# Gate and up of eight expert blocks as three fp32r terms, in a four-layer transformer stage

## The chip, the cores and the metric

The kernel runs on one core of a Trainium2 chip. The metric is device time in microseconds, the median of three runs. A profile of one execution stands beside it: it has every instruction's start and duration on each engine, the DMA issues, and the clock that TensorE was granted. Engines are named PE (TensorE), DVE (VectorE), ACT (ScalarE), POOL (GpSimd) and SP (SyncE, which here only issues DMAs).

## The reference

An activation of 4 x 256 tokens with 256 channels passes through four layers. Each layer forms a gated, decayed two-way scan ("cond") of the activation and feeds it to a feed-forward part, whose result is added. The third layer's feed-forward part is the one that matters here, a mixture of 8 experts with 2 chosen per token:

```python
def _L2_ffn_ref(hidden_states, gate_weight, gate_up_proj, down_proj):
    B, S, H, I, E, K = (4, 256, 256, 512, 8, 2)
    router_logits = x @ gate_weight.T
    probs = softmax(router_logits)
    top_v, top_i = top_k(probs, 2)
    ...
    def expert_step(acc, inp):
        gu, dp, w = inp
        gate, up = jnp.split(x @ gu.T, 2, axis=-1)
        hidden = silu(gate) * up
        y = hidden @ dp.T
        return (acc + w[:, None] * y, None)
```

The fourth layer's feed-forward part multiplies by three weight matrices that are first rounded to -1, 0 and 1 by their own mean ("ternary" weights).

## The kernel before

The eight experts' tokens are sorted by expert into blocks of 128 rows, at most 23 blocks (`NB`). The second expert loop works on one block at a time. A block `b` gathers its 128 rows from memory (POOL, `gather_block`), turns them on PE (`turn_block`) and copies them to `xbT` (ACT, `block_turned`). `gate` and `up` multiply `xbT` by the two halves of the expert's weights `gu`, 256 x 1024 numbers or 1 MB, which SP loads per block into a ring of three slots (`up_weights`, L375 to L379). ACT takes the silu of gate, DVE multiplies it by up (`block_h`), PE turns the product (`turn_block_hidden`) and multiplies it by the down weights (`block_down`), ACT copies the result out of PSUM (`block_y`), and POOL scatters it (`scatter_block`).

The order on each engine is written out by hand. On PE, iteration `b` is: gate of `b`, turning of the hidden rows of `b-1`, turning of the input rows of `b+1`, up of `b`, down of `b-1`. All operands of these matmuls are fp32; the profile shows each fp32 matmul as two records of the same shape.

DVE and POOL have other work in the same iterations. In the first 16 blocks DVE runs two scans per block for the fourth layer's cond (`late_scan`), POOL adds them up (`late_sum`, `late_value`), and every second block DVE takes a reciprocal and a product (`gain_reciprocal`, `gain_out`). And the three ternary weight matrices are prepared one after the other in one buffer, `traw` of 1 MB: SP loads it (`ternary_in`), DVE sums its magnitudes (`ternary_sum`, block 2, 8 or 14), PE adds over partitions (`ternary_total`) and DVE rounds (`ternary_round`, block 4, 10 or 16), DVE clips (`ternary_clip`, block 5, 11 or 17), and POOL writes the result as bf16 (`ternary_write`, block 6, 12 or 18). The next matrix can be loaded only after that write. SP's queue is in order: `ternary_in` of the second and third matrix stands right behind `up_weights(8)` and `up_weights(14)`, and it waits for the POOL write before it, so that `up_weights(9)` and `up_weights(15)` stand behind that wait:

```python
for b in range(2, NB):
    ...
    up_weights(b)
    if b in (8, 14):
        ternary_in((1, 8, 14).index(b))
```

In the first layer another expert loop already multiplies in three fp32r terms: with `mm3` each fp32 operand is given as a high part in fp32r and a low remainder, and high x high, high x low and low x high are added up.

Of the kernel before, what the change touches and what calls it, by code (L numbers as in the profile page):

```python
# [56 lines left out]
COPIED = {"": 0, "3": NT - 1}  # L57
LANED = 13
SUMMED = {"place": 1, "rows": 2, "dest": 3}
RANKED = [(0, 4, 0), (4, 2, 2), (6, 2, 3)]  # L60
# [8 lines left out]
def build(nc, x_d, kt_d, te_d, w_d, u_d, sm_d, gbias_d, down_d, fc2_d, w1_d, w2_d,  # L69
          q1_d, q1b_d, q2_d, q2b_d, rt_d, gu_d, dn_d, t1_d, t2_d, t3_d, cond_d, y_d, cw_d, out_d):  # L70
    with ExitStack() as ctx:
# [21 lines left out]
        kT = sb("kT", [P, NBLK, S])  # L93
        ekk = sb("ekk", [P, NBLK, 2, S])
        GT = sb("GT", [P, 2, NBLK, S])
        eu = sb("eu", [P, 2, 2, S])
        fw = sb("fw", [P, 2, 2, S])
        bw = sb("bw", [P, 2, 2, S])
        cond = sb("cond", [P, NT, C])
        turned = cursor[0]  # L100
# [12 lines left out]


        cursor[0] = turned
        cwb = sb("cwb", [P, CRING, TOK])
# [60 lines left out]
        gu = sb("gu", [P, RING, KC, 2 * I2])  # L177
        region2 = cursor[0]


# [7 lines left out]
        hm = sb("hm", [P, 2, I2])  # L188
        hT2 = sb("hT2", [P, 2, I2 // P, P])
        lane_of = sb("lane_of", [P, 2 * NT, P], F16)  # L190
        slab_of = sb("slab_of", [P, 2 * NT, NBW], F16)
        slab_val = sb("slab_val", [P, 2 * NT, NBW], F16)
        r2c = sb("r2c", [P, 2, NT, E2 * E2], BF16)
        xbT = sb("xbT", [P, 2, KC, P])
        slot_end = cursor[0]
        ends.append(cursor[0])


# [97 lines left out]
        def latent_bank(v):  # L296
            return bank[(4, 6, 2, 7)[v]]

        def unit(u):
# [15 lines left out]
        def _(sp):  # L315
# [16 lines left out]
            def expert_w1(eg):  # L332

                wait(sp, sem("w1_split"), eg - 1)
                sp.dma_start(w1raw[:, eg % 2, :], w1_d[:, eg, :]).then_inc(sem(f"w1_in{eg % 2}"), 16)
# [58 lines left out]
            for b in range(2, NB):  # L394
                if b == 2:
                    sp.wait_ge(sem("xb_in2"), 16)
                up_weights(b)
                if b in (8, 14):
                    ternary_in((1, 8, 14).index(b))
            sp.wait_ge(sem("y_out0"), 16 * ((NB + 1) // 2))  # L400
# [10 lines left out]
        def _(pool):  # L411
# [94 lines left out]
            def split_w1(eg):  # L506

                wait_alone(f"w1_in{eg % 2}", 16 * (eg // 2 + 1))
                wait_alone("z_ready", 8 * eg - 8)
                pool.tensor_scalar(w1hi[:, eg % 2, :], w1raw[:, eg % 2, :], 1.0, 0.0, ALU.mult, ALU.add).then_inc(sem("w1_high"), 1)  # L510
                wait_alone("w1_high", eg + 1)
                pool.tensor_tensor(w1lo[:, eg % 2, :], w1raw[:, eg % 2, :], w1hi[:, eg % 2, :].bitcast(F32), ALU.subtract
                                   ).then_inc(sem("w1_split"), 1)

# [104 lines left out]
            for b in range(NB):  # L619
                if b + RING < NB:  # L620
                    gather_block(b + RING)
                if b == 2:
                    pool.wait_ge(sem("routed"), ROUTED["dest"])
                if b >= 2:
                    scatter_block(b - 2)
                if b < 2 * NBLK:
                    late_sum(b // 2, 1 - b % 2, ("den", "num")[b % 2])
                    if b % 2 and b // 2 + 1 < NBLK:
                        late_value(b // 2 + 1)
                if b in (6, 12, 18):  # L630
                    ternary_write((6, 12, 18).index(b))
                if b in (19, 20):
                    combine_rows(b - 19)
# [50 lines left out]
        def _(act):  # L684
# [225 lines left out]
            def block_turned(b):  # L910

                act.wait_ge(sem("xbt_ready"), b + 1)
                wait(act, sem("up_done"), b - 1)
                act.activation(xbT[:, b % 2, :, :], xb_bank(b), ACT.Copy).then_inc(sem("xbT_ready"), 1)  # L914

# [92 lines left out]
        def _(dve):  # L1008
# [98 lines left out]
            def cond_low(n0, s, k):  # L1107
                n = n0 + 2 * s + k
                dve.wait_ge(sem("cT_high"), n + 1)
                dve.tensor_tensor(cTlo[:, k, HALF * s:HALF * s + HALF], cond_bank(n)[:],  # L1110
                                  cThi[:, k, HALF * s:HALF * s + HALF].bitcast(F32), ALU.subtract
                                  ).then_inc(sem("cT_low"), 1)

# [375 lines left out]
            def ternary_round(m):  # L1489
                dve.wait_ge(sem("tsum_ready"), m + 1)  # L1490
                dve.tensor_scalar(ws[:, 15 + m:16 + m], total_bank(4 + 6 * m), 1.0 / (C * HID), 1e-5, ALU.mult, ALU.max
                                  ).then_inc(sem("tsum_read"), 1)
# [13 lines left out]
            def late_scan(i, part):  # L1506
# [6 lines left out]
                else:  # L1513
                    dve.tensor_tensor_scan(bw[:, p, d, S - 2::-1], ekk[:, i, d, S - 1:0:-1], col(decf, n).to_broadcast([P, S - 1]),
                                           0.0, ALU.add, ALU.mult).then_inc(sem("scan_num" if part == 3 else "scan_den"), 1)

            for b in range(NB):
# [88 lines left out]
        def _(pe):  # L1606
# [22 lines left out]
            def turn_cond(l, n0, s):  # L1629
                pe.wait_ge(sem("cond_ready"), 4 * l + 2 * s + 2)  # L1630
                for k in range(KC):
                    n = n0 + 2 * s + k
                    wait(pe, sem("cT_low"), n - 1)
                    for j in range(TH):
# [95 lines left out]
            pe.wait_ge(sem("sm_low"), 2)  # L1730
            pe.wait_ge(sem("cT_low"), 2)
            scores_up(bank[6], E0, sm_hi, sm_lo, 0)
# [4 lines left out]
            shared_up(0)  # L1737
            pe.wait_ge(sem("cT_low"), 4)
            pe.wait_ge(sem("xl_low"), 1)
# [6 lines left out]
            def expert_z(u):  # L1746
# [6 lines left out]
                if u % 8 == 0:  # L1753
                    pe.wait_ge(sem("w1_split"), e // 4 + 1)
                mm3(bank[u % 4][:], (w1hi[:, slot, w], w1lo[:, slot, w]),
# [205 lines left out]
            def ternary_total(m):  # L1961
                pe.wait_ge(sem("tsum_part"), m + 1)
                pe.matmul(total_bank(4 + 6 * m), ones[:], ws[:, 9 + m:10 + m], start=True, stop=True).then_inc(sem("tsum_ready"), 1)

            def turn_block(b):

                pe.wait_ge(sem(f"xb_in{b % RING}"), 16 * (b // RING + 1))
                wait(pe, sem("xbT_ready"), b)
                for k in range(KC):
                    ins = pe.transpose(xb_bank(b)[:, k * P:k * P + P], xb[:, b % RING, k * P:k * P + P], ident[:])  # L1970
                ins.then_inc(sem("xbt_ready"), 1)

            def gate(b):
# [6 lines left out]
                wait(pe, sem("hm_ready"), b - 1)  # L1980
                if b in (4, 10, 16):
                    ternary_total((4, 10, 16).index(b))
                for k in range(KC):
                    ins = pe.matmul(bank[2 * (b % 2)][:], xbT[:, b % 2, k, :], gu[:, b % RING, k, 0:I2],  # L1984
                                    start=(k == 0), stop=(k == KC - 1))
                ins.then_inc(sem("gate_done"), 1)

            def up(b):

                if b == HALVED:  # L1990
                    pe.wait_ge(sem(f"gu_in{b % RING}"), 16)
                if b in (4, 10, 16):
                    pe.wait_ge(sem("tsum_read"), (4, 10, 16).index(b) + 1)
                for k in range(KC):
                    ins = pe.matmul(bank[2 * (b % 2) + 1][:], xbT[:, b % 2, k, :], gu[:, b % RING, k, I2:2 * I2],  # L1995
                                    start=(k == 0), stop=(k == KC - 1))
                ins.then_inc(sem("up_done"), 1)

# [149 lines left out]
```

## Time and profile before

| | |
|---|---|
| median of 3 runs | 446.32 us (446.3 to 446.4) |
| profiled execution, its own time | 446.5 us |
| its span, first to last instruction | 444.7 us |
| mean granted TensorE clock | 0.972 |
| PE busy | 400.8 us, 90% of the span |
| DVE busy | 328.9 us, 74% |
| POOL busy | 253.7 us, 57% |
| ACT busy | 236.9 us, 53% |
| bytes moved | 69.52 MB, mean 156 GB/s |

The second expert loop runs from about 248 to 384 us of the span. The profile's lists name a line of the kernel, an engine, an operation and the tiles that it writes and reads. L1984 is gate, L1995 is up, L2006 is the turning of the hidden rows, L2028 is down, L1504 is `block_h`, L1512 and L1514 are the late scans, L602, L606 and L597 are POOL's sums and value for them, L571 is the ternary write, L361 is the load of `traw` and L378 that of a block's weights. Ends of matmuls are modelled, so the pace of PE is read from starts.

### The profile page before, as it was taken

Reading aid. Unit: us, or ns where it says so; the run is one execution under the profiler, and the core shown is the slowest. Engines: PE = TensorE matmul, PEld = TensorE weight load, DVE = VectorE, ACT = ScalarE, POOL = GpSimd, SP = SyncE. Lnnn points to the kernel's source line nnn. Section 1 sums busy time; section 2 is a strip of 40 time slices with the busy share of each in tenths; the row PEclk is TensorE's granted clock in tenths of the full one; section 3 lists DMA queues with packets and bytes.
Section 4 is the critical chain, followed back from the end, with each engine's and each line's share of the span. In section 5 each row is a group of like instructions: output and inputs, shape, how many; then the busy total and the mean of one; then the engine's idle time right before and its main releaser. Section 6 shows DMA issues by size and latency. Waiting matters only on the chain.

```text
span 444.7 us, 6082 instructions
## 1 busy us (share of the span) xinstructions
PE 400.8 (90%) x1749; PEld 264.2 (59%) x1749; DVE 328.9 (74%) x620; ACT 236.9 (53%) x478; POOL 253.7 (57%) x352
## 2 busy tenths in 40 slices
PE   7798999999899999968894899999999999976895
PEld 7576788555455555636682466666666666653553
DVE  5998788999999999889978278548546411058993
ACT  6624683566676667658975222333333332249882
POOL 5474018578788997244622567876985562124641
PEclk9999999999999999997995999999999999999998
DMA  6910006366456656062023786496587760140011
GB/s 216 414 38 0 1 1 209 114 218 199 152 186 204 219 173 223 10 272 109 2 95 109 239 308 212 170 353 222 222 303 254 249 226 24 44 170 0 25 35 36
DMA packets 21439, 69.52 MB, mean 156 GB/s; under 512 B 3136, under 2 KB 7616, under 8 KB 17952
## 3 DMA queue, kind: packets, MB, share of 16 engines
q1 hardware_dynamic: 18112, 62.07, 39.8%
q0 software_dynamic: 2208, 6.03, 4.1%
q10 hardware_dynamic: 1088, 1.05, 0.7%
q8 instruction: 14, 0.23, 0.2%
q14 instruction: 17, 0.14, 0.1%
HBM read 63.90 MB, written 5.24 MB: 155 GB/s over the span
## 4 chain that ended last, share of the span: by engine, by line
PE 50%; DVE 27%; issue 12%; POOL 4%; ACT 3%; DMA 3%; SPq 0%; DVEq 0%; POOLq 0%; ACTq 0%
PE bank L1984 9%; PE bank L2028 9%; PE bank L1995 9%; PE bank L1764 5%; DVE hx L1289 5%; DVE fw L1078 4%; DVE bw L1081 3%; PE bank L1609 2%; PE bank L1611 2%; PE bank L1610 2%; PE bank L2006 2%; DVE fw L1086 2%; PE bank L1686 2%; DVE gl L1568 2%; PE bank L1861 2%
## 5 line engine op out<-in xcount | busy, mean ns | idle before, releaser
L1764 PE MATMUL bank<-hx,w2raw 128*128 128x512 f32 x128 | 67.2, 607 | 4.1 <-DVE hx L1289 3.3
L1504 DVE TENSOR_TENSOR hm<-bank,sl 128x512 f32<-128x512 f32 x23 | 15.8, 689 | 62.6 <-PE bank L1995 34.5
L802 ACT ACTIVATE rl<-bank 128x512 f32<-128x512 f32 x64 | 38.1, 595 | 38.8 <-PE bank L1611 37.7
L1609 PE MATMUL bank<-xlhi,w1hi 128*128 128x512 f32 x64 | 49.4, 772 | 0.0
L1289 DVE TENSOR_TENSOR hx<-bank,cwb 128x512 f32<-128x512 f32 x64 | 42.1, 660 | 3.1 <-ACT bank L806 3.1
L2028 PE MATMUL bank<-dn,hT 128*128 x184 | 43.6, 380 | 0.5 <-ACT hT L925 0.5
L1984 PE MATMUL bank<-gu,xbT 128*128 128x512 f32 x92 | 43.6, 596 | 0.5 <-ACT xbT L914 0.5
L2028 PEld LDWEIGHTS bank<-dn,hT 128*128 128x128 f32 x184 | 34.9, 190 | 14.8 <-issue 11.3
L1995 PE MATMUL bank<-gu,xbT 128*128 128x512 f32 x92 | 43.3, 593 | 0.0
L931 ACT ACTIVATE yb<-bank 128x256 f32<-128x256 f32 x23 | 8.8, 383 | 60.9 <-PE bank L2028 60.9
L583 POOL DMA_INDIRECT y_rows<-yb,dest_i x23 | 23.7, 1029 | 30.9 <-ACT yb L931 26.7
L1086 DVE RECIPROCAL fw<-fw 128x256 f32<-128x256 f32 x23 | 39.8, 1732 | 0.0
L806 ACT ACTIVATE bank<-rl 128x512 f32<-128x512 f32 x64 | 38.1, 597 | 0.0
L478 POOL TENSOR_TENSOR fw<-fw,bw 128x256 f32<-128x256 f32 x32 | 24.4, 761 | 15.6 <-DVE bw L1081 15.2
L919 ACT ACTIVATE sl<-bank 128x512 f32<-128x512 f32 x23 | 13.7, 597 | 33.5 <-PE bank L1984 33.5
L1764 PEld LDWEIGHTS bank<-hx,w2raw 128*128 128x128 f32 x128 | 22.4, 188 | 15.2 <-DVE hx L1289 9.7
L1078 DVE TENSOR_TENSOR_SCAN fw<-bank,ekk 128x256 f32<-128x256 f32 x46 | 31.1, 677 | 0.2
L576 POOL DMA_INDIRECT xb<-cond_rows,row_i x23 | 27.6, 1201 | 5.9 <-issue 1.9
L1081 DVE TENSOR_TENSOR_SCAN bw<-ekk,bank 128x255 f32<-128x255 f32 x46 | 30.8, 669 | 0.0
L475 POOL TENSOR_TENSOR eu<-eu,kT 128x256 f32<-128x256 f32 x16 | 11.7, 730 | 25.9 <-ACT eu L700 25.5
L482 POOL TENSOR_TENSOR fw<-fw,eu 128x256 f32<-128x256 f32 x32 | 23.7, 741 | 3.5
L1610 PE MATMUL bank<-xllo,w1hi 128*128 128x512 f32 x64 | 25.3, 395 | 0.0
(307 smaller groups left out, 955.2 us busy)
## 6 DMA issues: line engine op xcount, KB each, us to landing
gu<-in_gu SPq DMA_DIRECT2D x22, 1024.0 KB, 5.3
cwb<-cw_rows SPq DMA_DIRECT2D x32, 512.0 KB, 4.1
dn<-in_dn SPq DMA_DIRECT2D x4, 1024.0 KB, 7.8
traw<-in_t SPq DMA_DIRECT2D x3, 1024.0 KB, 5.0
w1raw<-in_w SPq DMA_DIRECT2D x8, 256.0 KB, 4.9
w2raw<-in_w SPq DMA_DIRECT2D x8, 256.0 KB, 4.4
kT<-in_kt SPq DMA_DIRECT2D x4, 256.0 KB, 4.5
x<-in_x SPq DMA_DIRECT2D x2, 512.0 KB, 7.0
```

Source lines behind the costliest of these rows:

```text
L802: act.activation(rl[:, u % 3, :], bank[u % 4][:], ACT.Relu).then_inc(sem("r_ready"), 1)
L806: act.activation(bank[u % 4][:], rl[:, u % 3, :], ACT.Square).then_inc(sem("sq_ready"), 1)
L1078: dve.tensor_tensor_scan(fw[:, p, d, :], decay(NBLK * l + blk, S), ekk[:, blk, d, :], 0.0, ALU.mult, ALU.add)
L1081: dve.tensor_tensor_scan(bw[:, p, d, S - 2::-1], ekk[:, blk, d, S - 1:0:-1], decay(NBLK * l + blk, S - 1), 0.0, ALU.add, ALU.mult).then_in ...
L1086: dve.reciprocal(fw[:, p, 1, :], fw[:, p, 1, :]).then_inc(sem("rden_ready"), 1)
L1289: dve.tensor_tensor(hx[:, 0, u % 4, :], bank[u % 4][:], cwb[:, e % CRING, HALF * s:HALF * s + HALF], ALU.mult).then_inc(sem("h0_ready"), 1)
L1609: pe.matmul(out, lhs[0], rhs[0], start=start, stop=False)
L1610: pe.matmul(out, lhs[0], rhs[1], start=False, stop=False)
L1764: pe.matmul(bank[4 + s][:], w2raw[:, e // 4 % 2, e % 4, :], hx[:, 0, u % 4, :], start=(e == 0), stop=(e == E0 - 1), skip_group_check=True) ...
L1984: ins = pe.matmul(bank[2 * (b % 2)][:], xbT[:, b % 2, k, :], gu[:, b % RING, k, 0:I2], start=(k == 0), stop=(k == KC - 1))
L1995: ins = pe.matmul(bank[2 * (b % 2) + 1][:], xbT[:, b % 2, k, :], gu[:, b % RING, k, I2:2 * I2], start=(k == 0), stop=(k == KC - 1))
L2028: ins = pe.matmul(y_bank(b), hT2[:, b % 2, j, :], own_down(b, j), start=(j == 0), stop=(j == 3))
```

## The change

In eight blocks, 6, 12 and 17 to 22, gate and up are computed with `mm3`. The high parts of the two halves of the weights are made by ACT (`weights_high`), one block ahead: the gate half at the start of its iteration, the up half after `block_turned`. DVE makes the low parts (`weights_low`, a subtraction that writes over the weights' own ring slot) and the low part of the rows (`block_low`, from PSUM); all of it stands around `block_h` of the block before. The high parts lie in two buffers over tiles that are idle then. The ternary steps move one block earlier: sums at blocks 1, 7 and 13, rounds at 3, 9 and 15, clips at 4, 10 and 16, writes at 5, 11 and 17, and the loads of the second and third matrix stand behind `up_weights(7)` and `up_weights(13)`. Some semaphores are merged and renamed.

```diff
+SPLIT = (6, 12, 17, 18, 19, 20, 21, 22)
+SUM_AT, ROUND_AT, CLIP_AT, WRITE_AT = (1, 7, 13), (3, 9, 15), (4, 10, 16), (5, 11, 17)
...
                 up_weights(b)
-                if b in (8, 14):
-                    ternary_in((1, 8, 14).index(b))
+                if b in SUM_AT[1:]:
+                    ternary_in(SUM_AT.index(b))
...
-                if b in (6, 12, 18):
-                    ternary_write((6, 12, 18).index(b))
+                if b in WRITE_AT:
+                    ternary_write(WRITE_AT.index(b))
...
+            def weights_high(b, up):
+
+                n = slice(up * I2, up * I2 + I2)
+                i = SPLIT.index(b)
+                act.wait_ge(sem(f"gu_in{b % RING}"), 16 * (b // RING + 1))
+                act.wait_ge(sem("up_done"), SPLIT[i - 2] + 1 if i >= 2 else 1)
+                act.activation(gu_high(b)[:, :, n], gu[:, b % RING, :, n], ACT.Copy).then_inc(sem("weights_high"), 1)
...
             for b in range(NB + 1):
+                if b + 1 in SPLIT:
+                    weights_high(b + 1, 0)
                 if b < NB:
                     block_silu(b)
...
                 if b + 1 < NB:
                     block_turned(b + 1)
+                if b + 1 in SPLIT:
+                    weights_high(b + 1, 1)
...
+            def weights_low(b, up):
+
+                n = slice(up * I2, up * I2 + I2)
+                dve.wait_ge(sem("weights_high"), halves_low(b, up))
+                dve.tensor_tensor(gul[:, b % RING, :, n], gu[:, b % RING, :, n], gu_high(b)[:, :, n].bitcast(F32), ALU.subtract
+                                  ).then_inc(sem("weights_low"), 1)
+
+            def block_low(b):
+
+                dve.wait_ge(sem("xbT_ready"), b + 1)
+                dve.tensor_tensor(xbl[:, b % 2, :, :], xb_bank(b).rearrange("p (k n) -> p k n", k=KC),
+                                  xbh[:, b % 2, :, :].bitcast(F32), ALU.subtract).then_inc(sem("turned_low"), 1)
+
             for b in range(NB):
-                if b in (4, 10, 16):
-                    ternary_round((4, 10, 16).index(b))
+                if b in ROUND_AT:
+                    ternary_round(ROUND_AT.index(b))
                 if b < 2 * NBLK:
                     late_scan(b // 2, 2 * (b % 2))
                     late_scan(b // 2, 2 * (b % 2) + 1)
+                if b + 1 in SPLIT:
+                    weights_low(b + 1, 0)
+                    block_low(b + 1)
                 block_h(b)
+                if b + 1 in SPLIT:
+                    weights_low(b + 1, 1)
                 if b >= 2 and b <= 2 * NBLK and b % 2 == 0:
                     gain_reciprocal(3 * NBLK + b // 2 - 1, (b // 2 - 1) % 2)
                     gain_out(3 * NBLK + b // 2 - 1, 3, b // 2 - 1, (b // 2 - 1) % 2)
...
-                if b in (2, 8, 14):
-                    ternary_sum((2, 8, 14).index(b))
-                if b in (5, 11, 17):
-                    ternary_clip((5, 11, 17).index(b))
+                if b in SUM_AT:
+                    ternary_sum(SUM_AT.index(b))
+                if b in CLIP_AT:
+                    ternary_clip(CLIP_AT.index(b))
...
+            def half_product(b, up):
+
+                n = slice(up * I2, up * I2 + I2)
+                for k in range(KC):
+                    if b in SPLIT:
+                        ins = mm3(bank[2 * (b % 2) + up][:], (xbh[:, b % 2, k, :], xbl[:, b % 2, k, :]),
+                                  (gu_high(b)[:, k, n], gul[:, b % RING, k, n]), k == 0, k == KC - 1)
+                    else:
+                        ins = pe.matmul(bank[2 * (b % 2) + up][:], xbT[:, b % 2, k, :], gu[:, b % RING, k, n],
+                                        start=(k == 0), stop=(k == KC - 1))
+                return ins
```

## Rows read from the trace of the kernel before

**Rows 1.** Busy time by stretch: window, length, then each engine's, clock, DMA.
```profile
248.50:380.00 131.50, 131.50 (x495) 81.99 (x496) 68.76 (x98) 39.99 (x110) 85.37 (x99) 1.00 0.65 230
...
433.50:436.90 3.40, 1.61 (x13) 1.07 (x11) 2.99 (x8) 1.46 (x4) 1.62 (x5) 1.00 0.04 15
436.90:440.30 3.40, 3.25 (x16) 2.74 (x16) 0.95 (x2) 0.93 (x3) 0.00 (x0) 0.51 0.08 27
```

**Rows 2.** Timeline of PE in the loop, blocks 16 to 18: start, length, instructions.
```profile
350.10 1.89 PE L2028 MATMUL bank<-dn,hT 128*128 x8
351.82 1.88 PE L1984 MATMUL bank<-gu,xbT 128*128 128x512 f32 x4
353.54 0.60 PE L2006 MATMUL bank<-ident,hm 128*128 128x128 f32 x4
...
354.20 1.88 PE L1995 MATMUL bank<-gu,xbT 128*128 128x512 f32 x4
```

**Rows 3.** Timeline of PE in the first layer's expert loop, one unit.
```profile
150.22 1.02 PE L1764 MATMUL bank<-hx,w2raw 128*128 128x512 f32 x2
...
151.55 0.40 PE L1611 MATMUL bank<-xlhi,w1lo 128*128 128x512 f32 x1
151.78 1.02 PE L1764 MATMUL bank<-hx,w2raw 128*128 128x512 f32 x2
```

**Rows 4.** Groups by line: count, busy us, mean ns. DVE subtractions' nearest, ACT's split.
```profile
L1247 DVE TENSOR_TENSOR rt<-rt 128x256 f32<-128x256 f32 x1 | 0.4, 426 | 0.0
L1230 DVE TENSOR_TENSOR rt<-rt 128x64 f32<-128x64 f32 x1 | 0.2, 228 | 0.0
L775 ACT ACTIVATE sm_hi<-sm_raw 128x1344 fp32r<-128x1344 f32 x1 | 1.3, 1307 | 0.0
```

**Rows 5.** Timeline of DVE in blocks 4 and 5 of the loop.
```profile
277.07 0.69 DVE L1512 TENSOR_TENSOR_SCAN fw<-dec,ekk 128x256 f32<-128x256 f32 x1
277.68 0.66 DVE L1514 TENSOR_TENSOR_SCAN bw<-ekk,dec 128x255 f32<-128x255 f32 x1
...
280.71 1.27 DVE L1498 TENSOR_SCALAR traw<-traw 128x2048 f32<-128x2048 f32 x1
```

**Rows 6.** Timeline of POOL in blocks 5 and 6 of the loop.
```profile
278.59 0.74 POOL L602 TENSOR_TENSOR fw<-fw,bw 128x256 f32<-128x256 f32 x1
...
280.16 0.73 POOL L597 TENSOR_TENSOR eu<-euk,kT 128x256 f32<-128x256 f32 x1
...
285.69 1.90 POOL L571 TENSOR_SCALAR tw<-traw 128x2048 bf16<-128x2048 f32 x1
```

**Rows 7.** Timeline of SP's DMA issues after the first ternary write.
```profile
287.61 0.34 SPq L361 DMA_DIRECT2D traw<-in_t  x1
288.71 3.45 SPq L378 DMA_DIRECT2D gu<-in_gu  x2
```

**Rows 8.** DMA landings: issues at 288.71 and 323.83, us from issue to landing.
```profile
gu<-in_gu SPq DMA_DIRECT2D x1, 1024.0 KB, 7.8
...
gu<-in_gu SPq DMA_DIRECT2D x1, 1024.0 KB, 9.9
```

**Rows 9.** Timeline of PE where the gate of block 8 starts.
```profile
293.20 1.88 PE L1984 MATMUL bank<-gu,xbT 128*128 128x512 f32 x4
```

**Rows 10.** Timelines of POOL and DVE in the first expert loop, two meetings.
```profile
148.04 1.00 POOL L478 TENSOR_TENSOR fw<-fw,bw 128x256 f32<-128x256 f32 x1
...
148.05 0.41 DVE L1092 SCALAR_TENSOR_TENSOR GT<-fw 128x256 f32<-128x256 f32 x1
...
89.02 0.98 DVE L1092 SCALAR_TENSOR_TENSOR GT<-fw 128x256 f32<-128x256 f32 x1
```

**Rows 11.** Timeline of DVE in block 16 of the loop.
```profile
344.65 0.69 DVE L1504 TENSOR_TENSOR hm<-bank,sl 128x512 f32<-128x512 f32 x1 [2.69 <-PE bank L1995]
345.26 1.74 DVE L1086 RECIPROCAL fw<-fw 128x256 f32<-128x256 f32 x1
347.11 0.42 DVE L1092 SCALAR_TENSOR_TENSOR GT<-fw 128x256 f32<-128x256 f32 x1
```

More of the change, by code:

```diff
@@ L94, in build @@
         ekk = sb("ekk", [P, NBLK, 2, S])
+        gt_at = cursor[0]
         GT = sb("GT", [P, 2, NBLK, S])
@@ L98, in build @@
         bw = sb("bw", [P, 2, 2, S])
+        cond_at = cursor[0]
         cond = sb("cond", [P, NT, C])
@@ L112, in build @@
         assert cursor[0] <= turned + KC * TOK * 4
+        cursor[0] = gt_at
+        guh0 = sb("guh0", [P, KC, 2 * I2], F32R)
+        assert cursor[0] <= gt_at + NBLK * S * 4
+        cursor[0] = cond_at
+        guh1 = sb("guh1", [P, KC, 2 * I2], F32R)
+        assert cursor[0] <= turned
         cursor[0] = turned
@@ L178, in build @@
         region2 = cursor[0]
+        cursor[0] = first_region
+        gul = sb("gul", [P, RING, KC, 2 * I2], F32R)
+        assert cursor[0] == region2
         cursor[0] = region
@@ L189, in build @@
         hT2 = sb("hT2", [P, 2, I2 // P, P])
+        lanes_at = cursor[0]
         lane_of = sb("lane_of", [P, 2 * NT, P], F16)
@@ L193, in build @@
         r2c = sb("r2c", [P, 2, NT, E2 * E2], BF16)
+        turned_at = cursor[0]
         xbT = sb("xbT", [P, 2, KC, P])
@@ L196, in build @@
         ends.append(cursor[0])
+        cursor[0] = turned_at
+        xbh = sb("xbh", [P, 2, KC, P], F32R)
+        assert cursor[0] == slot_end
+        cursor[0] = lanes_at
+        xbl = sb("xbl", [P, 2, KC, P], F32R)
+        assert cursor[0] <= lanes_at + 2 * NT * P * 2
         cursor[0] = first_region
@@ L297, in latent_bank, with gu_high, halves_low, rows_low @@
             return bank[(4, 6, 2, 7)[v]]
+        def gu_high(b):
+            return (guh0, guh1)[SPLIT.index(b) % 2]
+        def halves_low(b, up):
+            return EG + 2 * SPLIT.index(b) + up + 1
+        def rows_low(b):
+            return 4 + SPLIT.index(b) + 1
         def unit(u):
@@ L332, in expert_w1 @@
             def expert_w1(eg):
-                wait(sp, sem("w1_split"), eg - 1)
+                wait(sp, sem("weights_low"), eg - 1)
                 sp.dma_start(w1raw[:, eg % 2, :], w1_d[:, eg, :]).then_inc(sem(f"w1_in{eg % 2}"), 16)
@@ L509, in split_w1 @@
                 wait_alone("z_ready", 8 * eg - 8)
-                pool.tensor_scalar(w1hi[:, eg % 2, :], w1raw[:, eg % 2, :], 1.0, 0.0, ALU.mult, ALU.add).then_inc(sem("w1_high"), 1)
-                wait_alone("w1_high", eg + 1)
+                pool.tensor_scalar(w1hi[:, eg % 2, :], w1raw[:, eg % 2, :], 1.0, 0.0, ALU.mult, ALU.add).then_inc(sem("weights_high"), 1)
+                wait_alone("weights_high", eg + 1)
                 pool.tensor_tensor(w1lo[:, eg % 2, :], w1raw[:, eg % 2, :], w1hi[:, eg % 2, :].bitcast(F32), ALU.subtract
-                                   ).then_inc(sem("w1_split"), 1)
+                                   ).then_inc(sem("weights_low"), 1)
             split_w1(0)
@@ L913, in block_turned @@
                 wait(act, sem("up_done"), b - 1)
-                act.activation(xbT[:, b % 2, :, :], xb_bank(b), ACT.Copy).then_inc(sem("xbT_ready"), 1)
+                act.activation((xbh if b in SPLIT else xbT)[:, b % 2, :, :], xb_bank(b), ACT.Copy).then_inc(sem("xbT_ready"), 1)
+            def weights_high(b, up):
[4 more added lines that the diff above has]
+                act.activation(gu_high(b)[:, :, n], gu[:, b % RING, :, n], ACT.Copy).then_inc(sem("weights_high"), 1)
             def block_silu(b):
@@ L1111, in cond_low @@
                                   cThi[:, k, HALF * s:HALF * s + HALF].bitcast(F32), ALU.subtract
-                                  ).then_inc(sem("cT_low"), 1)
+                                  ).then_inc(sem("turned_low"), 1)
             def xl_low(s):
@@ L1490, in ternary_round @@
                 dve.wait_ge(sem("tsum_ready"), m + 1)
-                dve.tensor_scalar(ws[:, 15 + m:16 + m], total_bank(4 + 6 * m), 1.0 / (C * HID), 1e-5, ALU.mult, ALU.max
+                dve.tensor_scalar(ws[:, 15 + m:16 + m], total_bank(ROUND_AT[m]), 1.0 / (C * HID), 1e-5, ALU.mult, ALU.max
                                   ).then_inc(sem("tsum_read"), 1)
@@ L1515, in late_scan @@
                                            0.0, ALU.add, ALU.mult).then_inc(sem("scan_num" if part == 3 else "scan_den"), 1)
+            def weights_low(b, up):
+                n = slice(up * I2, up * I2 + I2)
+                dve.wait_ge(sem("weights_high"), halves_low(b, up))
+                dve.tensor_tensor(gul[:, b % RING, :, n], gu[:, b % RING, :, n], gu_high(b)[:, :, n].bitcast(F32), ALU.subtract
+                                  ).then_inc(sem("weights_low"), 1)
+            def block_low(b):
+                dve.wait_ge(sem("xbT_ready"), b + 1)
+                dve.tensor_tensor(xbl[:, b % 2, :, :], xb_bank(b).rearrange("p (k n) -> p k n", k=KC),
+                                  xbh[:, b % 2, :, :].bitcast(F32), ALU.subtract).then_inc(sem("turned_low"), 1)
             for b in range(NB):
-                if b in (4, 10, 16):
-                    ternary_round((4, 10, 16).index(b))
+                if b in ROUND_AT:
+                    ternary_round(ROUND_AT.index(b))
                 if b < 2 * NBLK:
@@ L1632, in turn_cond @@
                     n = n0 + 2 * s + k
-                    wait(pe, sem("cT_low"), n - 1)
+                    wait(pe, sem("turned_low"), n - 1)
                     for j in range(TH):
@@ L1730, in _ @@
             pe.wait_ge(sem("sm_low"), 2)
-            pe.wait_ge(sem("cT_low"), 2)
+            pe.wait_ge(sem("turned_low"), 2)
             scores_up(bank[6], E0, sm_hi, sm_lo, 0)
@@ L1737, in _ @@
             shared_up(0)
-            pe.wait_ge(sem("cT_low"), 4)
+            pe.wait_ge(sem("turned_low"), 4)
             pe.wait_ge(sem("xl_low"), 1)
@@ L1753, in expert_z @@
                 if u % 8 == 0:
-                    pe.wait_ge(sem("w1_split"), e // 4 + 1)
+                    pe.wait_ge(sem("weights_low"), e // 4 + 1)
                 mm3(bank[u % 4][:], (w1hi[:, slot, w], w1lo[:, slot, w]),
@@ L1962, in ternary_total @@
                 pe.wait_ge(sem("tsum_part"), m + 1)
-                pe.matmul(total_bank(4 + 6 * m), ones[:], ws[:, 9 + m:10 + m], start=True, stop=True).then_inc(sem("tsum_ready"), 1)
+                pe.matmul(total_bank(ROUND_AT[m]), ones[:], ws[:, 9 + m:10 + m], start=True, stop=True).then_inc(sem("tsum_ready"), 1)
             def turn_block(b):
@@ L1968, in turn_block @@
                 wait(pe, sem("xbT_ready"), b)
+                if b - 1 in SPLIT:
+                    pe.wait_ge(sem("turned_low"), rows_low(b - 1))
                 for k in range(KC):
@@ L1980, in gate @@
                 wait(pe, sem("hm_ready"), b - 1)
[L1981 to L1985, printed above, removed]
+                if b in ROUND_AT:
+                    ternary_total(ROUND_AT.index(b))
+                if b in SPLIT:
+                    pe.wait_ge(sem("turned_low"), rows_low(b))
+                    pe.wait_ge(sem("weights_low"), halves_low(b, 0))
+                ins = half_product(b, 0)
                 ins.then_inc(sem("gate_done"), 1)
@@ L1991, in up @@
                     pe.wait_ge(sem(f"gu_in{b % RING}"), 16)
[L1992 to L1997, printed above, removed]
+                if b in ROUND_AT:
+                    pe.wait_ge(sem("tsum_read"), ROUND_AT.index(b) + 1)
+                if b in SPLIT:
+                    pe.wait_ge(sem("weights_low"), halves_low(b, 1))
+                half_product(b, 1).then_inc(sem("up_done"), 1)
             def turn_block_hidden(b):
```

## The prediction, made before the changed kernel was run

> **What bounds the kernel now.** I read the busy time by stretch first. In the second expert loop PE is busy 131.5 of 131.5 us at full clock, while DVE is busy 69 and ACT 40 of them [rows 1]. The timeline of PE in one iteration then gives the pieces, by starts: down takes 1.72 us (350.10 to 351.82), gate 1.72, the two turnings together 0.66, up 1.72 like gate [rows 2]. That is 5.82 us per block with no gap, so a microsecond taken from PE here is a microsecond off the end, as long as operands come in time. Next I read what feeds PE: the issues on SP's queue with their landings [rows 7, 8], and the DVE and POOL instructions that decide when SP may issue [rows 5, 6].
>
> **What it removes on PE.** Gate is four fp32 records in 1.72 us, 0.43 each [rows 2]. For the new terms I use the first expert loop: one unit, two fp32 records and three fp32r terms, takes 151.78 - 150.22 = 1.56 us; less 0.86 for the two records this leaves 0.70, or 0.23 per term, and the last term's start to the next start is 0.23 too [rows 3]. Each of those terms loads its own weights, as the new ones do. Gate becomes six terms, 1.39 us, and saves 0.33; up the same. Eight blocks with two halves make 16 x 0.33 = 5.3 us. From below, a term whose weight load were not covered would eat the saving from 1.72 / 6 = 0.287 us on; no row has such a term. The Trainium skill ("TensorE: Matmul & The Clock Gate", Back-to-back issue gap) gives a pace of N/2.4 + 2.5 ns, 216 ns for 512 columns. By that figure the saving would be 16 x 0.42 = 6.8 us, and my sum 1.5 us less; the row has 0.23, and the measurement decides.
>
> **What it adds on ACT and DVE.** An ACT copy of 1344 elements per partition from fp32 to fp32r took 1.31 us [rows 4]; two of 1024 are 2.1 us per split block. A DVE operation with two SBUF inputs took 0.43 us for 256 elements and 0.23 for 64, 1.03 ns per element, so that 1024 take 1.22 us (estimate from these two rows) [rows 4]; two of these and 0.43 for `block_low` are 2.9 us. In blocks 17 to 22 DVE has little else, and a split block still takes PE 5.16 us: I cost this work at nothing there, covered by that time; without cover it would be at most DVE's sum, 0.7 + 2.9 us against 5.2, so still nothing. `weights_high` waits for the block's weights at the head of ACT's queue, with silu behind it; the weights land about a block earlier, so nothing.
>
> One place is tight. In iteration 16 DVE has, from the start of `block_h`: 0.69, `weights_low` 1.22, reciprocal 1.74, product 0.42, the clip of 1.27 that now stands here, `weights_low` 1.22 and `block_low` 0.43, together 7.0 us, or 6.6 if neighbours overlap as 344.65 to 345.26 do [rows 5, 11]. From there PE is ready for gate 18 after about 6.6 (1.72 + 1.39 + 0.66 + 1.39 + 1.72, less 0.3 that `block_h` starts late). The ternary write of 1.90 us [rows 6] may then hold up the next `weights_low`. I take a loss of 0.5 us, between 0.2 and 0.8.
>
> **What it moves: the weights of blocks 8 and 14.** This is where I expect the saving to go. The second ternary load now stands before `up_weights(8)` on SP. It waits for the POOL write of the first matrix, and that write waits for more than before. Step by step, on the clock of the trace before, whose blocks up to 5 keep their times:
> - The clip used to come in an iteration without reciprocal; now it comes in iteration 4, where the scans start today: 277.07 to 278.34. The scans of block 5 follow, ending 279.6 instead of 278.34 [rows 5].
> - POOL's sums and value for them stand before the write in iteration 5. They start 0.25 us after the scans and take 280.89 - 278.59 = 2.30, to 282.15; the write of 1.90 ends at 284.05, if nothing holds POOL up [rows 6].
> - Something does. When DVE ran a 0.41 us product of two SBUF tiles, a POOL sum that had started with it took 1.00 instead of 0.74 and ended 0.58 after DVE; where POOL came first, the same DVE product took 0.98 [rows 6, 10]. So the two wait for each other. `weights_low(6, 0)` runs from 279.5 to 280.75, right when POOL's first sum wants to start: it ends at 281.35 instead of 280.6, 0.75 late. `weights_low(6, 1)`, ready at about 281.6, slips in after the second sum and costs the value step another 0.95. The write ends at 285.75.
> - `traw` is issued then, and `up_weights(8)` 1.1 us behind it, at 286.85 [rows 7]. In this position the weights landed 7.8 and 9.9 us after issue, behind the megabyte of `traw` [rows 8]: 294.65 to 296.75. I take 8.3, 295.15, nearer the first.
> - Gate 8 starts at 293.20 today [rows 9]; block 6 brings it 0.66 forward, to 292.54. PE waits 2.6 us, between 2.1 and 4.2.
>
> The clip at 10, block 12 and `up_weights(14)` repeat this pattern. Two waits are 5.2 us (4.2 to 8.4). Before the change the same transfers had a block more of time.
>
> A wait of this length has a second price. In 433.5 to 436.9 PE was busy 1.61 of 3.4 us at full clock, and the next 3.4 us ran at 0.51, the lower level of 1.2 GHz [rows 1]. In those, PE does about 1.7 us less work. Of the two waits I let one be followed by such a fall: 1.7 us, between 0 and 3.4.
>
> The rule in the Trainium skill that speaks against this change is in "SBUF — State Buffer", Who interferes with whom: a DVE instruction with two SBUF inputs and a GpSimd instruction that reads SBUF exclude each other for the whole instruction, and `tensor_tensor` is named. By that rule the four steps above wait in full, 1.7 us per event as I have it; had the trace's meetings been a matter of the scalar product alone, the sum would be that of the first rival. No row here has a DVE `tensor_tensor` of that length beside POOL.
>
> **The sum.** -5.3 + 5.2 + 0.5 + 1.7 = +2.1 us. The profiled execution took 446.5 us itself (span 444.7 and 1.8 around it), so 448.6; it lies 0.2 over the median of the runs, 446.32, so the forecast for the median is 448.4. From the terms' bounds the forecast case goes from 445.4 (-5.3 + 4.2 + 0.2) to 453.6.
>
> **Rivals.**
> - *POOL isn't held up.* If `weights_low` and POOL's sums run side by side, the write ends at 284.05, the weights at 285.15 + 8.3 = 293.45 (292.95 to 295.05), and each wait is 0.9 us (0.4 to 2.5), too short for a fall of the clock. Then -5.3 + 1.8 + 0.2 = -3.3: 443.0, faster. For it: POOL's sum at 278.59 and later ones show a steady 0.72 to 0.74 beside other DVE work. Against it: the two meetings above. It decides from the point where both waits together stay under 4.8 us, that is, gate 8 starts before about 295.
> - *The weights come in time altogether.* Should `traw` and the weights both land within 6.8 us of the issue at 285.75, only the 0.2 remains: 441.2. The rows have 8.9 and 11.0 for such a pair (1.1 + 7.8 and 1.1 + 9.9), so it is unlikely.
> - *The backlog is as at 323.83, and both waits drop the clock.* 8.4 + 0.8 + 3.4 - 5.3 = +7.3: 453.6.
> - *The terms don't save what they should.* With 0.287 us per term nothing is gained and the late weights meet a PE that is no earlier: 2 x 2.0 + 0.5 = +4.5: 450.8. The 64 such units of the first loop speak against it.
>
> **How the numbers follow.** Forecast case 0.57, POOL not held up 0.23, weights in time 0.07, backlog with both falls 0.10, terms without gain 0.03. About 0.2%, 0.9 us, is what a measurement of this kernel can tell from no change, so "same" is 445.4 to 447.2. The first rival and the second give faster, 0.30. Of the forecast case some 0.12 lies within the bound (short waits, no fall), and 0.45 above; with the last two, slower is 0.58 and same 0.12. For 8 times in 10 the range leaves out the weights in time and the far part of the backlog case: 442.4 to 452.0. Since both signs are in it, the likeliest case's own: 446.3 to 450.6.
>
> **What would show it.** In the changed trace: gate and up of the eight blocks at 1.39 us by starts; the other pieces as they are. The write of the first matrix ending near 285.75 (284.05 for the first rival), POOL's first sum in block 5 near 1.5 us instead of 0.74. PE idle before the gates of blocks 8 and 14, ended by the DMA of `gu`, for 2.1 to 4.2 us each, and a small one at gate 18 ended by DVE. A clock of 0.5 right after at least one of these. The forecast is wrong if gate 8 starts within 1 us of the end of down 6, or if DVE keeps PE waiting in blocks 19 to 22.

## The result, and the profile after

The changed kernel takes 450.88 us, median of six runs (449.37 to 455.48); the kernel before took 446.36 in the same session (445.46 to 447.1). The ratio is 1.0115, 95% interval 1.0087 to 1.0144: slower by 4.5 us. The forecast was 448.4, within 442.4 to 452.0, slower more likely than not. The profiled execution is the longest of the six, 455.48 us (span 453.7, mean clock 0.965), so its waits are probably longer than those of the median run, which has no profile.

The matmuls themselves got cheaper, as worked out. The chain of waits of the changed kernel (start, length, piece) has gate 12, and before it gate 8:

```profile
291.32 1.73 PE bank L2105 x8
293.04 2.76 issue
...
319.50 1.73 PE bank L2105 x8
321.23 0.23 PE bank L1672
321.46 0.23 PE bank L1673
321.69 0.23 PE bank L1674
321.92 0.23 PE bank L1672
322.15 0.23 PE bank L1673
322.38 0.23 PE bank L1674
322.61 0.44 PE bank L2083 x4
```

L1672 to L1674 are the three terms, L2046 is the fp32 gate and up, L2105 down, L2083 the turning of the hidden rows, L2035 that of the input rows. Six terms take 1.38 us where four records took 1.72 [rows 2]. PE's timeline gives the whole period of a split block, by the starts of down in blocks 19 to 21:

```profile
372.73 1.89 PE L2105 MATMUL bank<-dn,hT 128*128 x8
377.85 1.89 PE L2105 MATMUL bank<-dn,hT 128*128 x8
382.98 1.89 PE L2105 MATMUL bank<-dn,hT 128*128 x8
```

5.13 us from one to the next, against 5.82 in [rows 2]: 0.69 saved per block. What spoils it are two stretches in which PE waits: the 2.76 us in the chain above, where [rows 9] had a gate that started on time, and one of 5.46 at gate 14. Busy time by stretch (window, length, then PE, weight loads, DVE, ACT, POOL, granted clock, DMA share, GB/s), to be held against the 131.5 busy of 131.5 us of [rows 1]:

```profile
248.50:389.00 140.50, 131.82 (x528) 89.60 (x529) 99.21 (x122) 55.56 (x127) 94.47 (x99) 0.96 0.61 215
292.50:296.00 3.50, 0.74 (x4) 0.37 (x3) 3.50 (x3) 0.38 (x1) 3.33 (x4) 1.00 1.04 426
295.97:299.40 3.43, 3.43 (x6) 1.25 (x6) 0.57 (x1) 0.03 (x1) 2.95 (x4) 0.50 0.98 408
333.50:336.90 3.40, 0.00 (x0) 0.00 (x0) 2.19 (x3) 0.38 (x1) 2.94 (x4) 1.00 1.02 378
336.93:343.76 6.83, 6.13 (x12) 3.36 (x13) 0.00 (x0) 1.62 (x4) 3.14 (x4) 0.50 0.48 198
```

After each wait the clock stands at 0.50, the level of 1.2 GHz: for 3.43 us, then for 6.83. With PE 9.56 of these 10.26 us busy at half pace, about 4.8 us more went there.

SP's queue shows why. L394 is the load of `traw`, and the first L411 behind each is the load of the weights of block 8 or 14:

```profile
286.34 0.34 SPq L394 DMA_DIRECT2D traw<-in_t  x1
287.44 1.44 SPq L411 DMA_DIRECT2D gu<-in_gu  x2
...
325.49 0.34 SPq L394 DMA_DIRECT2D traw<-in_t  x1
326.58 4.39 SPq L411 DMA_DIRECT2D gu<-in_gu  x3
```

By the trace's landing marks the weights were there at 295.71 and 337.54, that is 8.3 and 11.0 us after their issues; gates 8 and 14 start right behind (PE's timeline, idle time before in brackets):

```profile
295.80 1.89 PE L2046 MATMUL bank<-gu,xbT 128*128 128x512 f32 x2 [2.76 <-issue]
...
337.63 2.05 PE L2046 MATMUL bank<-gu,xbT 128*128 128x512 f32 x2 [5.46 <-issue]
```

And the issue of `traw` is late because POOL ends its write (L604) at 286.3. Timelines of DVE and POOL around it, to be held against [rows 5, 6]; L1557 and L1559 are the scans, L1566 `weights_low`, L1549 `block_h`, L635, L639 and L630 POOL's sums and value:

```profile
279.16 0.66 DVE L1559 TENSOR_TENSOR_SCAN bw<-ekk,dec 128x255 f32<-128x255 f32 x1
279.74 1.20 DVE L1566 TENSOR_TENSOR gul<-gu,guh 128x1024 fp32r<-128x1024 f32 x1
...
281.78 1.70 DVE L1566 TENSOR_TENSOR gul<-gu,guh 128x1024 fp32r<-128x1024 f32 x1
283.40 1.21 DVE L1557 TENSOR_TENSOR_SCAN fw<-dec,ekk 128x256 f32<-128x256 f32 x1
```

```profile
279.90 1.62 POOL L635 TENSOR_TENSOR fw<-fw,bw 128x256 f32<-128x256 f32 x1 [1.15 <-DVE bw L1559]
281.67 0.72 POOL L639 TENSOR_TENSOR fw<-fw,eu 128x256 f32<-128x256 f32 x1
282.36 1.71 POOL L630 TENSOR_TENSOR eu<-euk,kT 128x256 f32<-128x256 f32 x1
284.05 2.27 POOL L604 TENSOR_SCALAR tw<-traw 128x2048 bf16<-128x2048 f32 x1
```

The sum that met the first `weights_low` took 1.62 us, the value that met the second 1.71, against 0.73 to 0.74 in [rows 6]; the one between them kept its 0.72. It works in both directions: the second `weights_low` took 1.70 instead of 1.20, and the scan that followed 1.21 instead of 0.68, behind POOL's value.

### The profile page after: what moved, and what is told of

Same layout as the page of the kernel before. It is cut to its first block, busy times and chain, and to the rows that moved or that the text cites. A ratio compares the mean times of both kernels' runs of the same rounds, so it can differ in the third digit from the quotient of the medians.

```text
span 453.7 us, 6207 instructions
## 1 busy us (share of the span) xinstructions
PE 401.5 (89%) x1781; PEld 272.4 (60%) x1781; DVE 359.9 (79%) x644; ACT 251.7 (55%) x494; POOL 262.5 (58%) x352
## 4 chain that ended last, share of the span: by engine, by line
PE 49%; DVE 28%; issue 13%; ACT 3%; POOL 3%; DMA 3%; SPq 0%; DVEq 0%; POOLq 0%; ACTq 0%
PE bank L2046 12%; PE bank L2105 9%; PE bank L1827 5%; PE bank L1672 4%; DVE hx L1334 4%; PE bank L1674 4%; PE bank L1673 4%; DVE fw L1123 4%; DVE bw L1126 3%; DVE fw L1131 2%; PE bank L2083 2%; DVE xp L1392 2%; PE bank L1749 2%; DVE gl L1631 2%; PE bank L1896 1%
## 5 line engine op out<-in xcount | busy, mean ns | idle before, releaser
L2046 PE MATMUL bank<-gu,xbT 128*128 128x512 f32 x120 | 60.9, 633 | 8.7 <-issue 8.2
L1672 PE MATMUL bank<-xlhi,w1hi 128*128 128x512 f32 x64 | 49.3, 771 | 0.0
L2105 PE MATMUL bank<-dn,hT 128*128 x184 | 43.5, 379 | 0.5 <-ACT hT L966 0.5
L1549 DVE TENSOR_TENSOR hm<-bank,sl 128x512 f32<-128x512 f32 x23 | 15.7, 683 | 35.5 <-issue 25.5
L2105 PEld LDWEIGHTS bank<-dn,hT 128*128 128x128 f32 x184 | 34.8, 190 | 11.7 <-issue 7.4
L2046 PEld LDWEIGHTS bank<-gu,xbT 128*128 128x128 f32 x120 | 22.4, 201 | 26.5 <-issue 25.2
L609 POOL DMA_INDIRECT xb<-cond_rows,row_i x23 | 25.9, 1128 | 8.6 <-PE bank L2035 4.0
L1566 DVE TENSOR_TENSOR gul<-gu,guh 128x1024 fp32r<-128x1024 f32 x16 | 21.1, 1325 | 5.9 <-ACT guh L955 5.9
```

What stands on the lines that cost most here:

```text
L609: pool.indirect_dma_start(xb[:, b % RING, :], None, cond_d, bass.IndirectOffsetOnAxis(ap=row_i[:, b:b + 1], axis=0)).then_inc(sem(f"xb_in{ ...
L1672: pe.matmul(out, lhs[0], rhs[0], start=start, stop=False)
L2046: ins = pe.matmul(bank[2 * (b % 2) + up][:], xbT[:, b % 2, k, :], gu[:, b % RING, k, n], start=(k == 0), stop=(k == KC - 1))
L2105: ins = pe.matmul(y_bank(b), hT2[:, b % 2, j, :], own_down(b, j), start=(j == 0), stop=(j == 3))
```

## The experiments

Times are medians; the kernel before had 446.56 us in the session of the first four and 445.76 in that of the other three, and ratios are to it.

**Only SP's order.** Everything of the change stays, but the second and third ternary load go back behind the weights of blocks 8 and 14.

```diff
-                if b in SUM_AT[1:]:
-                    ternary_in(SUM_AT.index(b))
+                if b in (8, 14):
+                    ternary_in((1, 8, 14).index(b))
```

> Only SP's order is changed: the loads of the second and third ternary matrix stand behind the weights of blocks 8 and 14 again, not ahead of them; all else is the changed kernel. Theory (the weights of blocks 8 and 14, queued behind the load that waits for POOL's write, come late): both waits of PE, 2.8 and 5.5 us in the profiled execution, and the clock's falls behind them are gone, and what is left is the saving of 5.3 us less some 0.5 at gate 18: 441.5 us, between 440.8 and 443. The weights of blocks 9 and 15 now stand behind the wait and have 5.8 us more time; if they still came late it would show as a wait of up to 1 us at gate 15. Rival (DVE's and ACT's new work holds up PE, and the DMA is only what was waited for last): the order on SP changes little, 449 to 451 us.

Measured: 441.56 us (440.56 to 442.95), ratio 0.988 (0.9858 to 0.9901). It beats both kernels. POOL's write still starts late and ends at 286.03, but `up_weights(8)` was issued at 280.25 and gate 8 follows down without a gap (POOL's, SP's and PE's timelines, then busy time by stretch):

```profile
283.77 2.26 POOL L604 TENSOR_SCALAR tw<-traw 128x2048 bf16<-128x2048 f32 x1
```

```profile
280.25 0.34 SPq L411 DMA_DIRECT2D gu<-in_gu  x1
286.06 0.34 SPq L394 DMA_DIRECT2D traw<-in_t  x1
```

```profile
290.87 1.89 PE L2105 MATMUL bank<-dn,hT 128*128 x8
292.60 1.88 PE L2046 MATMUL bank<-gu,xbT 128*128 128x512 f32 x4
```

```profile
248.50:379.00 130.50, 129.82 (x543) 90.27 (x544) 100.18 (x122) 55.84 (x130) 98.13 (x100) 1.00 0.66 233
```

PE is busy 129.8 of 130.5 us at full clock, and gate 14 has no wait either. So the two lines on SP's queue are the whole loss: without them the change gives 5.0 us.

**POOL's cover removed.** For blocks 6 and 12 `weights_low` reads a PSUM bank in place of the SBUF tile, so that it has one SBUF input.

```diff
+                whole = gu[:, b % RING, :, n]
+                if b in (6, 12):
+                    whole = bank[2 * (b % 2) + up][:].rearrange("p (k n) -> p k n", k=1).to_broadcast([P, KC, I2])
-                dve.tensor_tensor(gul[:, b % RING, :, n], gu[:, b % RING, :, n], ...
+                dve.tensor_tensor(gul[:, b % RING, :, n], whole, ...
```

> In blocks 6 and 12 alone the DVE subtraction of the low weights takes its first operand from a PSUM bank instead of the weights in SBUF, so the low parts there are not the weights' (that part of the computation is left out); size, count and waits are the same. Theory (a DVE instruction with two SBUF inputs and POOL's instructions wait for each other): POOL's first sum in iteration 5 falls from 1.62 to 0.74 us, the value step from 1.71 to 0.73, the write from 2.27 to about 1.9; the write ends at about 284.1 instead of 286.3, and the waits at gates 8 and 14 are each shorter by about 2.2 us, with fewer falls of the clock: 445 to 447 us. Rival (POOL is slowed by something else, or the write is not what the weights wait for): POOL's instructions keep their lengths and the time stays at 450 to 451.

Measured: 443.65 us (442.35 to 444.87), ratio 0.9927 (0.9905 to 0.9949), a little better than expected. POOL's four steps have their old lengths (POOL's timeline), and the write ends 2.8 us earlier than in the changed kernel:

```profile
279.36 0.73 POOL L635 TENSOR_TENSOR fw<-fw,bw 128x256 f32<-128x256 f32 x1 [1.15 <-DVE bw L1559]
280.24 0.73 POOL L639 TENSOR_TENSOR fw<-fw,eu 128x256 f32<-128x256 f32 x1
280.93 0.72 POOL L630 TENSOR_TENSOR eu<-euk,kT 128x256 f32<-128x256 f32 x1
281.64 1.89 POOL L604 TENSOR_SCALAR tw<-traw 128x2048 bf16<-128x2048 f32 x1
```

`weights_low` itself takes 1.20 and 1.21 us there (DVE's timeline), so DVE is as busy beside POOL as in the changed kernel:

```profile
279.20 1.20 DVE L1569 TENSOR_TENSOR gul<-bank,guh 128x1024 fp32r<-128x1024 f32 x1
...
281.24 1.21 DVE L1569 TENSOR_TENSOR gul<-bank,guh 128x1024 fp32r<-128x1024 f32 x1
```

The weights of block 8 landed at 292.36, and gate 8 started within 0.2 us of when PE was due. At gate 14 PE still waited (PE's timeline), without a fall of the clock:

```profile
328.28 1.96 PE L2049 MATMUL bank<-gu,xbT 128*128 128x512 f32 x4 [1.15 <-issue]
```

So it is the second SBUF input of `weights_low` that held POOL up, not DVE's being busy. This is the rule of the Trainium skill that the prediction weighed ("SBUF — State Buffer", Who interferes with whom), and its other half as well: a DVE instruction with at most one SBUF input, outside the two-port modes, doesn't contend with GpSimd. The trace agrees with both, 1.62 and 1.71 against 0.73 and 0.72.

**The moved steps alone.** The ternary steps and their loads are moved, no block is split.

```diff
-SPLIT = (6, 12, 17, 18, 19, 20, 21, 22)
+SPLIT = ()
```

> No block is split; what stays of the change is the ternary steps one block earlier, with the SP order of the changed kernel. Theory: the write ends at about 284.4, as nothing new meets POOL, and the weights of block 8 are issued at 285.5 and land between 293.3 and 295.4, while the gate is ready at 293.7 (no block 6 that saves): waits of 0 to 2 us at gates 8 and 14 and at most one fall of the clock: 447 to 450 us, slower than before with nothing added. Rival (the cost comes from the split's own work): 446.4, as before.

Measured: 446.52 us (445.28 to 447.3, 12 runs), ratio 0.9992 (0.9977 to 1.0007). The expectation missed: the move costs nothing by itself. The rival's number came out, but not for its reason: with all eight blocks split and only the order on SP put back, 441.56 was measured. POOL's value and write still meet DVE's scans and take 1.10 and 2.26 us, but the write ends at 284.98 (POOL's timeline); the weights landed 7.1 us after their issue, at 293.25, and PE was due for gate 8 at 293.73, since block 6 was not shortened (PE's timeline). About half a microsecond was left.

```profile
281.64 1.10 POOL L630 TENSOR_TENSOR eu<-euk,kT 128x256 f32<-128x256 f32 x1
282.72 2.26 POOL L604 TENSOR_SCALAR tw<-traw 128x2048 bf16<-128x2048 f32 x1
```

```profile
293.73 1.88 PE L2046 MATMUL bank<-gu,xbT 128*128 128x512 f32 x4
```

**The six late blocks alone.** Blocks 6 and 12 are not split; the moves stay.

```diff
-SPLIT = (6, 12, 17, 18, 19, 20, 21, 22)
+SPLIT = (17, 18, 19, 20, 21, 22)
```

> Blocks 6 and 12 are not split, 17 to 22 are. Theory: the waits at gates 8 and 14 are those of the kernel without any split (0 to 2 us each), and six blocks save 0.66 us each less 0.5 at gate 18: 3.5 us below the kernel with the ternary steps moved and no split, 443.5 to 446.5 us. So the two blocks 6 and 12 cost more than they save. Rival (each split block costs by its own work): the six blocks are six eighths of the loss, 449.5 us.

Measured: 443.35 us (442.13 to 444.57), ratio 0.9918 (0.9896 to 0.994), just below what was expected. Against the moved steps alone the six blocks save 3.2 us. By the starts of down, six times 0.69 less 0.64 that is lost in block 18 (5.77 us instead of 5.13, shown in the next section) would be 3.5, as expected; the difference is within what these runs scatter. PE's timeline shows the first part of that loss, before gate 18:

```profile
353.54 0.47 PE L1672 MATMUL bank<-guh,xbh 128*128 128x512 f32 x1 [0.26 <-issue]
```

Adding blocks 6 and 12 with the loads moved makes 450.88 of it; with the loads behind, all eight take 441.56. The same two splits cost 7.5 us in one order and save 1.8 in the other, if the order is worth nothing while they aren't split; the moved steps alone took as long as the kernel before, which speaks for it, but the six late blocks weren't run with the loads behind.

**POOL's write first.** As the change, but in iterations 5, 11 and 17 the write stands ahead of the sums and the value.

```diff
+                if b in WRITE_AT:
+                    ternary_write(WRITE_AT.index(b))
                 if b < 2 * NBLK:
                     late_sum(b // 2, 1 - b % 2, ("den", "num")[b % 2])
 ...
-                if b in WRITE_AT:
-                    ternary_write(WRITE_AT.index(b))
```

> SP's order as in the change (the second and third ternary load ahead of the weights of blocks 8 and 14), all eight blocks split; only POOL's ternary write stands ahead of the scans' sums and value in iterations 5, 11 and 17. Theory (the issue is late because the write stands behind POOL's sums, which DVE's subtractions hold up): the clip ends near 278.6, the write runs beside the scans and ends between 280.8 and 282, the weights of block 8 are issued by 283.1 and land by 291.5, before PE wants them near 293; no wait at gates 8 and 14 and no fall of the clock in the loop: 441.5 to 443 us (the reciprocal of block 6 now gets its sums some 2 us later, up to 1 us). Rival (one megabyte ahead of the other on the queue is enough to make the weights late, whenever it is issued): PE still waits 1 us or more at gates 8 and 14: 445 to 450.

Measured: 444.19 us (442.39 to 445.08, 12 runs), ratio 0.9956 (0.9938 to 0.9973): above the theory's range, below the rival's. The mechanism came out as expected: the write ended at 280.15, the weights of block 8 landed at 288.40, and PE waited at neither gate 8 nor 14. But the exclusion now works against DVE. The write holds up the second scan, 2.31 us instead of 0.66, `weights_low` comes later, and PE waits for DVE at gate 6, 1.09 us, and as long again at gate 12. I had not priced that. The profile is of the fastest of the 12 runs, 442.39 us; what the median run lost beyond these two waits isn't shown. POOL's, DVE's and PE's timelines:

```profile
278.01 2.14 POOL L604 TENSOR_SCALAR tw<-traw 128x2048 bf16<-128x2048 f32 x1
```

```profile
278.38 2.31 DVE L1559 TENSOR_TENSOR_SCAN bw<-ekk,dec 128x255 f32<-128x255 f32 x1
```

```profile
282.39 0.47 PE L1672 MATMUL bank<-guh,xbh 128*128 128x512 f32 x1 [1.09 <-DVE xbl L1572]
```

**One of the two loads.** The second ternary load stands behind the weights of block 8, the third ahead of those of block 14.

```diff
-                if b in SUM_AT[1:]:
-                    ternary_in(SUM_AT.index(b))
+                if b in (8, 13):
+                    ternary_in((1, 8, 13).index(b))
```

> As the change, but the second ternary load stands behind the weights of block 8 again; the third stays ahead of those of block 14. Theory (two independent waits of like price, each with its fall of the clock): half of the 9.3 us between the changed kernel (450.9) and the one with both loads behind (441.6): 446 us, 444.5 to 447.5; no idle PE at gate 8, 2 to 5.5 us at gate 14. Rival (the wait at gate 14 is a consequence of the one at gate 8): no wait at either, 441.6 to 442.5. Second rival (the wait at gate 14 is the dear one, 5.5 against 2.8 in the one profile): 447.5 to 449.

Measured: 445.23 us, ratio 0.9984 (0.9954 to 1.0014), with a wide spread: the eleven runs that the ratio rests on go from 442.4 to 448.93, and a twelfth took 450.56. The profiled execution took 445.16, close to the median. Gate 8 has no wait, gate 14 has one of 3.27 us, and the clock falls behind it (PE's timeline, busy time by stretch):

```profile
330.26 2.20 PE L2046 MATMUL bank<-gu,xbT 128*128 128x512 f32 x3 [3.27 <-issue]
```

```profile
330.97:334.38 3.41, 3.41 (x9) 1.83 (x8) 0.00 (x0) 1.03 (x3) 2.80 (x4) 0.50 0.98 408
```

The wait at gate 14 doesn't need the one at gate 8. By ratios the one load accounts for 0.0104 of the 0.0235 between the kernels with none and with both: near half, as for two waits of like price. The second rival, the wait at gate 14 as the dear one, is not what the medians show.

**Nothing moved.** All eight blocks are split, every ternary step stands where it stood before.

```diff
-SUM_AT, ROUND_AT, CLIP_AT, WRITE_AT = (1, 7, 13), (3, 9, 15), (4, 10, 16), (5, 11, 17)
+SUM_AT, ROUND_AT, CLIP_AT, WRITE_AT = (2, 8, 14), (4, 10, 16), (5, 11, 17), (6, 12, 18)
```

> All eight blocks split, and every ternary step back where it was before the change: sums at 2, 8 and 14, rounds at 4, 10 and 16, clips at 5, 11 and 17, writes at 6, 12 and 18, loads behind the weights of blocks 8 and 14. It asks whether the splits need the moved steps at all. Theory (the order on SP's queue alone decides): no wait at gates 8 and 14; iterations 5, 11 and 16 or 17 have the clip or the round beside the subtractions on DVE, 1.3 us more, which PE's 5.2 to 5.8 us per block cover in part: 442 to 444 us. Rival (DVE has no room for the clip and the subtractions in one iteration): PE waits for DVE 1 us or more at the gates of blocks 6, 12 and 18: 444.5 to 447.

Measured: 441.93 us (440.79 to 444.28), ratio 0.9908 (0.9882 to 0.9934), the same as with SP's order alone within the intervals. The profiled execution is the longest of its six, 444.28 us. The clip fits beside the subtractions in iteration 5, and block 6 still takes PE 5.14 us by the starts of down. The write one block later meets no scan and keeps its 1.90 us (POOL's timeline); a wait of 0.81 us remains at gate 15 (PE's timeline), whose weights stand behind the third load here. The splits need none of the moved steps.

```profile
288.25 1.90 POOL L604 TENSOR_SCALAR tw<-traw 128x2048 bf16<-128x2048 f32 x1
```

```profile
334.79 1.95 PE L2046 MATMUL bank<-gu,xbT 128*128 128x512 f32 x4 [0.81 <-issue]
```

## Why the prediction was right, and by how much it was off

- *Saving of the terms, 5.3 us.* Right. 0.23 per term, 0.69 per block by the period. With the loss at gate 18 the prediction had 4.8 net; with SP's order put back 5.0 was measured. By the Trainium skill's 216 ns for 512 columns ("TensorE: Matmul & The Clock Gate", Back-to-back issue gap) the saving would be 1.5 us more, an estimate from the page's figure; the trace doesn't agree, its terms start 0.23 us apart.
- *Work on ACT and DVE at nothing in blocks 17 to 22.* Right but for block 18: blocks 19 to 21 keep PE's 5.13 us period, and PE waits for nothing in block 22. `weights_low` takes 1.20 to 1.23 us where nothing holds it up; the estimate had 1.22.
- *Gate 18, 0.5 us (0.2 to 0.8).* Right, in place and in size. The idle time of 0.26 us before gate 18, seen in the run with the six late blocks, is one part of it. By the starts of down in the changed kernel block 18 takes 5.77 us instead of 5.13, 0.64 more: its gate starts late, and so does its up (first term at 366.11). Its `weights_low` took 1.98 us beside POOL's third write, which is the hold-up that the prediction named. PE's timeline:

```profile
361.82 1.89 PE L2105 MATMUL bank<-dn,hT 128*128 x8
...
366.11 0.50 PE L1672 MATMUL bank<-guh,xbh 128*128 128x512 f32 x1
...
367.59 1.89 PE L2105 MATMUL bank<-dn,hT 128*128 x8
```

- *POOL held up.* Right, step by step: the first sum took 0.88 us longer (0.75 predicted), the value 0.98 longer (0.95 predicted). The write ended at 286.3 instead of 285.75: it started 0.2 us later than worked out (284.05 for 283.85), and beside a scan it took 2.27 where I had left it at 1.90. The first rival (POOL not held up) is what the PSUM variant makes real: forecast 443.0, measured 443.65. What the prediction held to be for that rival was misread: POOL's sum at 278.59 had no DVE work beside it, since DVE stood idle from 278.34 until `block_h` at 280.10, and `block_h` has one of its inputs in PSUM (DVE's timeline of the kernel before):

```profile
280.10 0.69 DVE L1504 TENSOR_TENSOR hm<-bank,sl 128x512 f32<-128x512 f32 x1 [1.76 <-issue]
```

- *Weights of blocks 8 and 14 late.* Right at gate 8: 8.3 us from issue to landing, a wait of 2.76 for 2.6. At gate 14 of the profiled execution it was 11.0 us and a wait of 5.46, beyond the bound of 4.2 that the two landings in [rows 8] gave. But that execution is the longest of six; in the kernel with one load, profiled close to its median, the same load took 8.8 us and PE waited 3.27.
- *One fall of the clock, 1.7 us.* Mis-sized: one fall was taken for the two waits. Both were followed by a fall, and so was the one wait of the kernel with one load. In the profiled execution the second fall was twice as long, and the two cost about 4.8 us.

The forecast was +2.1 us, the medians differ by +4.5: within the stated range, and 0.3 us above the likeliest case's own (446.3 to 450.6). The two waits and the falls were put at 6.9 us; with 5.0 saved elsewhere they come to 9.5. A wait with a fall of 3.4 us at half pace behind it is 2.76 + 1.7 = 4.5 us at gate 8, and 3.27 + 1.7 = 5.0 in the kernel with one load; two of them would be 9.0 to 10.0. So the term that was too small is, by this estimate, mainly the second fall, 1.7 of the missing 2.6 us, which the prediction had only in its rival with both falls; the rest is waits somewhat longer than 2.6. In the profiled execution the late landing at gate 14 comes on top: 8.2 of waiting and 4.8 of slow clock make 13.0, and its 455.48 us lies 13.9 above the kernel with SP's order put back.

What stays open: why the weights that stand right behind a ternary load land after 6.8 us in one execution and after 11.0 in another. In the changed kernel at 326.58 and in the kernel with one load at 321.40 SP's loads around them are the same, and they landed after 11.0 and 8.8 us. The trace has sixteen landing marks for each of these loads. In both, fifteen had come after 8.0 to 8.1 us; the last came 2.9 us later in the first, 0.8 in the second. One coincidence holds in all nine profiles, with two such loads in each. Where the load took 8.5 us or more (six loads), a packet of the instruction queue q8, of 0.02 MB, was moved 2.4 to 7.7 us after its issue. Where the load took 8.3 us or less (twelve loads), none came before 9.8 us. That the packet is the cause isn't shown, and it took only about 1 us itself. The scatter of the landings is a likely source of the spread in the kernel with one load; no run tells what drives it.

## What to carry to other kernels

When a transfer is put ahead of another on one queue, ask what it waits for: the operands queued behind it inherit that wait, and here two swapped lines turned a gain of 5.0 us into a loss of 4.5. Before adding DVE work with two SBUF inputs, look for POOL work in the same stretch and follow both ways, which POOL step ends later and which DVE step, if the order is turned round, ends later instead. A cover of half a microsecond, as the moved steps alone left it, is not a cover once the consumer is made faster.

## What the runs showed of the hardware

Idle stretches of PE of 0.81, 1.09 and 1.15 us in the loop were followed by no change of the granted clock; those of 2.76, 3.27 and 5.46 us were followed by 3.43, 3.41 and 6.83 us at 0.50. And the scans count as well in the exclusion with POOL: one of 0.66 us took 2.31 beside POOL's write. In the kernel without any `weights_low`, POOL's value took 1.10 us and its write 2.26, beside scans that took 0.99 and 1.14 instead of 0.68 and 0.66.
